# Joint block of residual, first read and cross attention: projections and rotations of the first heads placed among the residual's last steps

## What is computed

```python
x = x + attn(layernorm(x), ...)              # its sum is finished in the joint block
h = layernorm(x)
def rat_read(res, W, gamma, beta, n):        # "read": 4 channels -> n outputs, then a norm of each
    y = einsum('blhc,hoc->bloh', res.reshape(b, l, H, C), W)
    return ((y - mean(y)) * rsqrt(var(y) + EPS)) * gamma + beta
q, k, v = split(rat_read(h, ..., 3), 3)
q, k, v = q @ Wq.T, k @ Wk.T, v @ Wv.T       # 256 x 256 each
q, k = rope(q, pos), rope(k, pos)            # 16 heads of 16 features
p = softmax(mask(q @ k.T / sqrt(16)));  o = p @ v
```

## Time and profile before

| what | us |
|---|---|
| median of three runs | 1807.92 |
| the three runs | 1806.28, 1807.92, 1808.39 |
| the profiled execution, its own time | 1809.05 |
| the profiled execution, its span | 1807.3 |
| VectorE's last `rd.finish` starts | 1248.59 |
| first load of the ring is issued | 1262.04 |
| first product of the attention loop | 1272.19 |

### The profile page before, as it was taken

One profiled execution on the slowest core, in us unless ns is written; L12 is line 12 of the kernel. 1 busy time (PEld: TensorE's weight loads), 2 busy tenths in 40 slices (PEclk: granted clock), 3 DMA queues, 4 the chain that ended last, 5 costly groups with the idle time before them and its releaser, 6 DMA issues. The chain is left out here.

```text
span 1807.3 us, 21042 instructions
## 1 busy us (share of the span) xinstructions
PE 1594.4 (88%) x6880; PEld 1051.9 (58%) x6880; DVE 1357.9 (75%) x2078; ACT 909.9 (50%) x1682; POOL 578.4 (32%) x463
## 2 busy tenths in 40 slices
PE   4899999999999999999999988677889766888999
PEld 3466666666666666666666665465456445445444
DVE  7788888888888887887887766784578679568881
ACT  3355554454554555455554544244268876457630
POOL 2246446446445455455455454101110100000000
PEclk9999999999999999999999999888789856798999
DMA  4002101111111111111110010321544200010121
GB/s 182 24 24 59 35 24 58 36 29 54 36 36 47 36 47 36 35 48 35 36 47 24 24 35 12 120 99 44 108 84 57 90 1 0 1 35 1 47 76 41
DMA packets 30963, 84.20 MB, mean 47 GB/s; under 512 B 6006, under 2 KB 7304, under 8 KB 30600
## 3 DMA queue, kind: packets, MB, share of 16 engines
q1 hardware_dynamic: 30856, 82.87, 15.9%
HBM read 70.27 MB, written 12.58 MB: 46 GB/s over the span
## 5 line engine op out<-in xcount | busy, mean ns | idle before, releaser
L518 DVE SCALAR_TENSOR_TENSOR acc<-pj,sc_o,acc 128x1024 f32<-128x1024 f32 x232 | 293.8, 1279 | 89.6 <-PE pj L649 86.1
L628 POOL TENSOR_TENSOR prob<-prob,inv_total 128x512 f32<-128x512 f32 (+3 forms) x256 | 189.6, 745 | 384.7 <-DVE inv_total L560 384.7
L518 DVE SCALAR_TENSOR_TENSOR q_acc<-pj,sc_q,q_acc 128x1024 f32<-128x1024 f32 x224 | 286.3, 1278 | 34.3 <-PE pj L649 29.0
L649 PE MATMUL pj<-ctx_hi,w_o 128*128 128x512 f32 x528 | 237.1, 449 | 25.5 <-ACT spare L407 12.2
L649 PE MATMUL pj<-zT_hi,w_q 128*128 128x512 f32 x512 | 225.4, 440 | 4.1 <-PEq L81 3.1
L649 PE MATMUL pj<-ctx_lo,w_o 128*128 128x512 f32 x528 | 208.0, 394 | 0.0
L461 ACT ACTIVATE prob<-ps,low_max 128x512 f32<-128x512 f32 (+3 forms) x256 | 134.1, 526 | 144.5 <-DVE low_max L553 144.4
L649 PE MATMUL pj<-zT_lo,w_q 128*128 128x512 f32 x512 | 204.4, 399 | 0.0
L703 PE MATMUL ps<-kT,qT 128*128 128x512 f32 (+3 forms) x512 | 185.6, 445 | 10.4 <-ACT prob L461 10.4
L727 PE MATMUL pv<-probT,v 128*128 128x512 f32 (+3 forms) x512 | 169.4, 433 | 0.0
L649 PEld LDWEIGHTS pj<-ctx_hi,w_o 128*128 128x128 f32 x528 | 99.1, 188 | 110.6 <-DVE acc L518 43.1
(11 more groups left out here) (332 smaller groups left out, 3152.6 us busy)
## 6 DMA issues: line engine op xcount, KB each, us to landing
raw_o<-in_w_o SPq DMA_DIRECT2D x33, 512.0 KB, 3.6
raw_q<-in_w_q SPq DMA_DIRECT2D x32, 512.0 KB, 3.6
x_ring<-qk_kept SPq DMA_DIRECT2D x64, 128.0 KB, 5.0
ln_x<-in_x SPq DMA_DIRECT2D x8, 512.0 KB, 7.0
raw_kv<-in_w_k SPq DMA_DIRECT2D x8, 512.0 KB, 3.5
raw_kv<-in_w_v SPq DMA_DIRECT2D x8, 512.0 KB, 4.1
x<-in_x SPq DMA_DIRECT2D x8, 512.0 KB, 7.2
x_kept<-x SPq DMA_DIRECT2D x8, 512.0 KB, 2.9
```

Source lines behind the costliest of these rows:

```text
L518: dve.scalar_tensor_tensor(out=dst, in0=pj[slot][:], scalar=scale, in1=dst, op0=ALU.mult, op1=ALU.add).then_inc(evac_v, 1)
L628: pool.tensor_tensor(prob[:, k % PROBS, 0:w], prob[:, k % PROBS, 0:w], inv_total[:, n:n + 1].to_broadcast([P, w]), ALU.mult).then_inc(norm ...
L649: ins = pe.matmul(pj[slot][:, b * S:(b + 1) * S], lhs, part[:, b * S:(b + 1) * S], start=n == 0, stop=n == 1)
```

## The change

TensorE: `project(0)` and `project(1)` move one step of the loop earlier, to the ends of i = 7 and i = 8; `project(2)` goes to the head of i = 9, before `turn_y(7)`; `project(3)` follows the loop, ahead of `project_v(7)`. VectorE: `rope(0)` and `rope(1)` go to the heads of i = 8 and i = 9, where `residual` stood in earlier steps, and `low(0)` goes to the end of i = 8. ScalarE: `high(0)` and `high(1)` go behind `copy_h` and ahead of `copy_y` in i = 8 and i = 9, and three waits that stood ahead of `high(0)` go behind the loop, ahead of `rows(0)`. SyncE and GpSimd keep their lists. No instruction is added or removed.

```diff
@@ TensorE, loop over i
+                if i == NT + 1:
+                    project(2)
                 if i >= 2:
                     ...
                     rd.turn_y(pe, i - 2, before_last=(lambda v=i - 3: project_v(v)) if i >= 3 else None)
-                if i >= NT:
-                    project(i - NT)
+                if NT - 1 <= i <= NT:
+                    project(i - NT + 1)
+            project(3)
             project_v(NT - 1)
-            project(2)
-            project(3)
@@ VectorE
             for i in range(NT + 2):
                 if i < NT:
                     residual(i)
+                else:
+                    rope(i - NT)
...
                 if i >= 2:
                     rd.finish(dve, link, i - 2)
-                if i >= NT:
-                    rope(i - NT)
-                if i == NT + 1:
+                if i == NT:
                     low(0)
             low(1)
@@ ScalarE
                 if 1 <= i <= NT:
                     rd.copy_h(act, i - 1)
+                if i >= NT:
+                    high(i - NT)
...
                     rd.copy_y(act, i - 2)
                 if i >= 3:
                     copy_v(i - 3)
-                if i == NT:
-                    act.wait_ge(sel_made, 2)
-                    act.wait_ge(moved, 16 * NT)
-                    act.wait_ge(done, NT)
-                if i >= NT:
-                    high(i - NT)
+            act.wait_ge(sel_made, 2)
+            act.wait_ge(moved, 16 * NT)
+            act.wait_ge(done, NT)
             rows(0)
```

## The result

The changed kernel took 1802.2 us (median of 20 runs, 1797.36 to 1806.42), the kernel before beside it 1810.36 us (20 runs, 1801.42 to 1817.23): ratio 0.9954, 95% interval 0.9943 to 0.9965. Timed again on another occasion (12 runs beside 23) it was 0.9974, 0.9957 to 0.9992. Both say faster, by 5 to 8 us. The profiled execution has a span of 1802.3 us, 5.0 shorter than before. Of these 8.4 us, 2.9 lie behind the block of the change, where nothing differs; that part takes 382.4 to 387.0 us over all the traces of this document, so it is chance.

What follows compares the result with a forecast made beforehand. The attention's start was taken to wait for the ring's loads, with `low(3)` close behind. Profiled 1809.05 minus 4.2 (between -3.6 and -5.1) gave 1804.85, less 1.1 for the median: 1803.7 us, range 1802.5 to 1804.6.

Steps and rivals of the forecast that it cites:

- What bounds it: Start of attention: the first product waits for the ring's loads; a second way through `low(3)` has 3.06 us slack.
- the ring: Loads behind round 1's last store: the first product could start at 1266.8 instead of 1272.19, allowing at most -5.4 us.
- Round 0 into step 8: `project(0)` and `rope(0)` go ahead of tile 7's chain on VectorE and delay it; cost 5.45 us.
- Rounds 1 to 3: Store and loads 5.4 us earlier, `project(2)` hidden, `low(3)` ending last; first maximum at 1269.5 instead of 1273.13, -3.6 us.
- the third rival: Tail before the attention: projects at low clock behind TensorE's new gap add up to 9.5 us; +5.9, 1813.8 us; chance 0.13.
- The 3.04 from `turn_y(7)` to the next project: TensorE, before `project(3)`: 3.04 us taken over from a low-clock stretch, putting its start at 1258.5; gives -3.6 us.
- the forecast's other bound: TensorE at the full level between `turn_y(7)` and `project(3)`: 1.5 us in place of 3.04, giving -5.1 us.
- So I carry the whole shift to the end: Attention loop: it moves whole with its earlier start, so all of the 4.2 us taken reaches the end.
- The clock gives more: Group 0's units: a higher granted clock saves another 3.6 us; -7.8 in all, 1800.1 us; chance 0.12.
- The shift is given back: Attention loop: low-clock stretches fall differently and cost 3 us; -1.2 in all, 1806.7 us, no change; chance 0.30.
- The tail gets longer: Projects before the attention run at low clock, delaying `copy_v(7)` and `low(3)`; +5.9 us, 1813.8 us; chance 0.13.

Runs made afterwards that it cites:

- the experiment with ScalarE's tail: Changed kernel with ScalarE's tail reordered to rows 0, high 2, copy_v 7, high 3, rows 1, rows 2; ratio to the kernel before 0.9972.
- the kernel with six products: Kernel before plus six unused 128x512 products in TensorE's 6.27 us wait for the ring's loads; ratio 0.9980.
- twelve products: Kernel before plus twelve unused 128x512 products on TensorE between project 3 and the first unit of scores; ratio 0.9996.

## Why the prediction was right

The forecast was 1803.7 us with a gain of 4.2; measured were 1802.2, and gains of some 8 and 5 us. That the time fits better than the gain is luck: it was worked out from three runs of the kernel before (1807.92), and the twenty beside the changed kernel gave 1810.36. Had the forecast started from those, it would have been some 4 us too high.

*What bounds it* held. Of two ways that end at the first maximum, the ring and `low(3)`, the forecast had the second one last, by 2.7 us. In the trace it is last by 0.75, and the experiment with ScalarE's tail freed 0.8.

*Round 0 into step 8* held, a little dearer: `turn_h(7)` is 6.5 to 6.7 us late in place of 5.9, as `project(0)` started 8.2 us behind `turn_h(6)` (1236.25) in place of the 7.4 worked out; the products ahead of it (line 875) took 3.70 us there, 3.39 before. Some half of this is the price of the rotation's place on VectorE, as its list of before under the other two shows: `turn_h(7)` is then 3.6 us late (12.33 against 8.71), and the start gains 7.2 us more.

*Rounds 1 to 3* held in their order, and in their sum by luck: two terms were wrong and nearly cancelled. `turn_y(7)` starts at 33.0 and 32.8 in place of the 30.9 worked out, as `products(7)`, behind the new gap of 3.61, took 3.73 us in place of the 2.45 taken over from before, on top of the 0.6 to 0.9 us from round 0. This is in small what the third rival put down to that gap, and it is why the ring came later than forecast. The 3.04 from `turn_y(7)` to the next project was 1.58, as the forecast's other bound had it (1.5). The rest is as written: `low(1)` follows `rd.finish(7)` at once (line 1373 at 1260.89 behind line 911), `project(2)` lies in the wait, ScalarE's chain behind `project_v(7)` sets the last low part, and the first maximum comes 3.0 to 3.5 us earlier; 3.6 was worked out and 4.2 taken.

*"So I carry the whole shift to the end"* is the step that was mis-sized, by 2.5 us in the first part of the loop, toward the good side: the loop is not a fixed length behind its start. Where low clock falls in it differs between the orders, and this kernel lost a stretch that the kernel before has in both traces. The rows of the clock that the forecast shows leave out 1284 to 1320 us, where it lies. In the rest of the loop the traces differ by up to 3.7 us by chance. It did not have to go this way. TensorE's list alone starts 6.2 us early and by its trace loses about half of it in the first part of the loop.

*The rivals.* "The clock gives more" named the mechanism and the wrong place: group 0's units stay at 0.50, the gain came 26 us behind the first maximum. In the kernel with six products, where that rival's condition was made, the clock was back at 0.50 four us behind the first maximum, group 0's part took as long as before, and the 2.8 us that the loop lost came from the middle stretch. So the 3.6 put on that rival had no support there; with twelve products that part was 0.7 shorter (13.67).

The rule of the Trainium skill that the forecast cited there ("TensorE: Matmul & The Clock Gate", "What's actually happening": activity releases the throttle) agrees with the middle stretch, which is at 1.00 in all six traces with added products. It does not agree with group 0's units: TensorE is busy for 11.65 of 12 us there and stays at 0.50. With twelve products ahead, it is granted 1.00 in the first four us of these units and 0.50 from the sixth to the twelfth, in which it is busy for 5.88 of 6. The measurement decides: in these rows the clock fell, and stayed low, while TensorE was busy.

"The shift is given back" did not happen here, but in part did for VectorE's list of before (first part of the loop 3.1 us longer than before) and for TensorE's alone (2.9). "The tail gets longer" did not, but for `products(7)`: `project(1)`, `(2)` and `(3)` all ran at or near the full level, 1.88 to 1.95 per half.

What stays open: why the same idle 1.60 us is followed by a low stretch in four of the orders and not in the changed kernel or with ScalarE's tail in another order. That it can be removed is shown, and what it costs; what selects it is not.

## What to carry to other kernels

A start that comes earlier is not a finish that comes earlier: where TensorE bounds a loop and the granted clock has two levels, read the clock of the loop in both traces before a gain or a loss is put down to the moved work. To find where time went, take a row that returns in the loop, here `turn_max`, and compare its distances in the traces, two of each kernel: what does not repeat is chance. Ahead of work that many wait for, an engine should not stand waiting for a round of side work; here the rotation belongs behind `rd.finish`, worth 7 us at the start. Where an idle gap of TensorE is followed by a low stretch, a few products of no use in the gap are a cheap test, and may be kept if the time falls; of the versions with them here, only the one with six is clear of noise against its own kernel.

## What the runs showed of the hardware

Six unused products in a gap of TensorE made the kernel before 0.2% faster (0.9980, 0.9969 to 0.9990); three in the kernel with VectorE's list of before took it from 0.9948 to 0.9927, within noise. The stretch of low clock that they remove costs 3.1 us of 13 (12.96 against 9.83). A 128x512 product of 32-bit floats takes 0.86 us at the full level (six of the profile's rows in 2.79 us, 24 in 10.46), not the 0.43 that one row of the timeline suggests. So a project is two times two products, each shown as two rows, and not two times four. And of two traces of the same kernel, one can have a loop 3.7 us longer with the same start, which is more than the 3.0 to 3.5 us by which this change moved it.
